# Attention row sums inverted on GpSimd by a power of minus one, in a fused attention and expert kernel

## Chip, cores and metric

The kernel runs on one core of one Trainium2 chip. The metric is the device time of one execution in microseconds (us). Before the change it is 942.04 us, the median of 3 runs (941.04 to 942.63).

## What is computed

```python
xn = layernorm(x)                                # x: 8 batches x 1024 tokens x 128
q, k = xn @ Wq.T + bq, xn @ Wk.T + bk            # 8 heads x 2
v = xn @ Wv.T + bv                               # 8 heads x 16
scores = leaky_relu(q @ k.T / sqrt(2), 0.2)      # per batch and head, 1024 x 1024
out = softmax(scores) @ v
y = x + (gamma * out + xn) + experts(xn)
```

`experts` is a top-2 routed layer of 16 experts with a capacity of 1024 tokens each; 12 of them are two matmuls with a gelu between. The change touches only the division of the softmax: each row of exponentials times values is divided by the sum of its exponentials.

## The kernel before

A prologue (0 to about 127 us) normalizes the tokens, projects q, k and v, routes the tokens and writes split bf16 parts of q and k to DRAM. Then attention and experts take turns: attention of batches 0 to 2, the 12 experts (about 365 to 540 us), attention of batches 3 to 7.

Attention is cut into 32 **passes** (`p`, 0 to 31): a pass is one batch, one group of 4 heads and one half (512) of its queries. A pass has 16 **units** (`i`): 8 chunks of 128 keys, and for each chunk two pairs of heads. One unit is a tile of 128 keys by 1024 (2 heads x 512 queries), in one of three slots of a ring in PSUM, and goes through four steps:

- `scores(i)`, TensorE, L825: two matmuls. It waits until the exponentials of unit i-3 have left the slot.
- `rectify(i)`, VectorE, L1133: max with 0 and a factor, in place in PSUM.
- `shifted(i)`, TensorE, L835: two matmuls that add the linear part and a shift onto it.
- `exponentials(i)`, ScalarE, L718: exp from the slot into SBUF (`pr`).

TensorE runs `shifted(i)`, `scores(i+2)`, and then `values` (L855), half of exponentials times values for the chunk before, in this order, unit by unit. `values` adds up into one of two PSUM banks (`acc`), 16 values and the row sum in each block of 32 rows, since the value tile has a column of ones.

When a pass is complete, VectorE does `turn(p)` (L1109): a 32x32 block transpose of `acc` into the SBUF tile `ot`, put ahead of `rectify` of the sixth unit (`TURN = 5`) of the pass after it. Ahead of the seventh it does `denominators(p)` (L1115): the reciprocal of the 16 row sums per partition, into `rg`. GpSimd then multiplies in `quotient(p)` (L439, `att`), and the sync engine's queue (SP) issues `spread(p)`: 16 small DMAs (L333, 8 KB each) that bring the blocks to their tokens in `moved`. One pass later GpSimd adds `moved` to `y` in `add_attention(p)` (L452), which `settle` calls. The last pass of each of the two attention parts (p = 11 and 31, `LAST`) goes another way: ScalarE copies `acc`, TensorE transposes it (L866), and VectorE's `finish` inverts (L1122) and multiplies (L1125) straight into `moved`. It does so before and after the change.

GpSimd's order is written out by hand, one program: in the first attention part `scatter` issues 128 indirect DMAs (L490, tokens to the experts' inputs), 11 or 12 in each pass but the last; in the second part `gather` issues 128 indirect DMAs (L505) and combines them (L518, L525), 4 or 8 a pass and none in the last. Each indirect DMA waits in `paced` for a certain unit's exponentials. In each pass, between these, stands `results`: `settle(p - 2)`, then `quotient(p - 1)`. So the quotient of a pass and all that follows on GpSimd are one queue. SP's queue is one too: operand loads (L312 to L314) every second pass, spreads, stores of finished batches to `out` (L323), and at the change to the experts `load_expert` (L357), which waits for all scatters. What TensorE needs first of the experts are the tokens of expert 0 and 1 (`turn_rows`, L898).

```python
                    def results():
                        ...
                        if p > first + 1:
                            settle(p - 2)
                        if p > first:
                            quotient(p - 1)
```

Of the kernel before, what the change touches and what calls it, by code (L numbers as in the profile page):

```python
# [8 lines left out]
ALU = mybir.AluOpType  # L9
# [3 lines left out]
P = 128  # L13
# [4 lines left out]
H, DV, DQ = 8, 16, 2  # L18
HG = 4
# [5 lines left out]
HALF = 512  # L25
# [29 lines left out]
UP = TB * PAIRS  # L55
# [5 lines left out]
TURN = 5  # L61
BLOCK = 32
NR = P // BLOCK
# [38 lines left out]
def build(nc, x, consts, w_qk, b_qk, w_vr, b_v, r_b, n_w, n_w_row, w1t, b1, w2t, b2, cvec, gamma, out):  # L102
# [4 lines left out]
    with ExitStack() as ctx:  # L107
        def sb(name, shape, dt=F32):
            return ctx.enter_context(nc.sbuf_tensor(name, shape, dt))

        def sem(name):
            return ctx.enter_context(nc.semaphore(name))
# [38 lines left out]
        vp = sb("vp", [P, NHG, TB, HG, 32])  # L151
        pr = sb("pr", [P, BUFS, HG, HALF])
        ot = sb("ot", [P, 2, HALF])
        rg = sb("rg", [P, 2, HALF // BLOCK])
        att = sb("att", [P, 2, NR, GT, DV])
        moved = sb("moved", [P, 2, HG, GT, DV])
        rowones = sb("rowones", [1, M], BF16)
# [42 lines left out]
                 "v_rdy y_upd hi_rdy rem_rdy mid_rdy lo_rdy scaled v_evac lg_rdy lgb_rdy parts_out0 parts_out1 dir_rdy ext_rdy "  # L200
                 "kmax_rdy bok_rdy hat1_rdy hat_rdy u_rdy ub_rdy shift_rdy shift_out0 shift_out1 "
                 "qz_init weighted at_rdy sum_rdy inv_rdy row_step route ones_rdy max_rdy off_rdy reset_rdy r_exp cnt_rdy pos_rdy ztile init_rdy kz_init "
                 "ld0 ld1 vp_rdy s1 relu s2 exps pv acc_evac o_rdy turned rg_rdy att_rdy spread0 spread1 y_att "
                 "scat staged pool_step carry "
                 "ed0 ed1 etr edt fc1 gel fc2 yo_rdy yo_out gath0 gath1 comb final").split()
        S = {n: sem(n) for n in names}
# [6 lines left out]
        def wait_done(engine, name, count):  # L213

            if not (isinstance(count, int) and count <= 0):
                engine.wait_ge(S[name], count)
# [27 lines left out]
        LAST = (BH * NPB - 1, B * NPB - 1)  # L244

        def quotients(p):

            return sum(k not in LAST for k in range(p + 1))

        def spreads(p):  # L250

            return sum(k not in LAST and k % 2 == p % 2 for k in range(p + 1))
# [137 lines left out]
        def _(pool):  # L390
            pool.memset(onesb[:], 1.0)
            pool.memset(ef[:, 3, :], 0.0).then_inc(S["ztile"], 1)
            pool.memset(rowones[:], -1.0)
            pool.memset(va[:, :, :, DV:DV1], 1.0)
            pool.memset(vp[:], 0.0).then_inc(S["init_rdy"], 1)
            pool.memset(kz[:].rearrange("p a e m -> p (a e m)").bitcast(F32), 0.0)
# [34 lines left out]

            def quotient(p):

                pool.wait_ge(S["rg_rdy"], p + 1)
                if p > 1:
                    wait_done(pool, f"spread{p % 2}", 16 * HG * NR * spreads(p - 2))
                rows = ot[:, p % 2, :].rearrange("p (t r c) -> p t r c", r=NR, c=BLOCK)[:, :, :, 0:DV]
                inv_rows = rg[:, p % 2, :].rearrange("p (t r) -> p t r", r=NR).unsqueeze(3)
                pool.tensor_tensor(att[:, p % 2, :, :, :].rearrange("p r t d -> p t r d"), rows,  # L439
                                   inv_rows.broadcast_to([P, GT, NR, DV]), ALU.mult).then_inc(S["att_rdy"], 1)  # L440

# [105 lines left out]
            def attention(b0, b1, move):  # L547
                first, last = b0 * NPB, b1 * NPB - 1
                for p in range(first, last + 1):
                    b = p // NPB  # L550

                    def results():

                        if p % NPB == 0:
                            value_rows(b, 1)
                        if p % NPB == NQ and b + 1 < B:
                            value_rows(b + 1, 0)
# [5 lines that stand above are left out]
                    move(p, results)  # L563
                settle(last - 1)
                settle(last)
# [376 lines left out]
        def _(dve):  # L942
# [161 lines left out]
            def turn(p):  # L1104

                dve.wait_ge(S["pv"], TB * (p + 1))
                if p > 1:
                    dve.wait_ge(S["att_rdy"], quotients(p - 2))
                dve.transpose(ot[:, p % 2, :], acc[p % 2]).then_inc(S["turned"], 1)  # L1109

            def denominators(p):

                dve.wait_ge(S["turned"], p + 1)
                rows = ot[:, p % 2, :].rearrange("p (q c) -> p q c", c=BLOCK)
                dve.reciprocal(rg[:, p % 2, :], rows[:, :, DV]).then_inc(S["rg_rdy"], 1)  # L1115

            def finish(p):

                dve.wait_ge(S["o_rdy"], 1 + LAST.index(p))
                rows = acc[p % 2].rearrange("p (t g c) -> p g t c", g=HG, c=BLOCK)  # L1120
                inv_rows = rg[:, p % 2, :].rearrange("p (g t) -> p g t", g=HG)
                dve.reciprocal(inv_rows, rows[:, :, :, DV]).then_inc(S["rg_rdy"], 1)  # L1122
                dve.wait_ge(S["rg_rdy"], p + 1)
                dve.wait_ge(S["y_att"], p - 1)
                dve.tensor_tensor(moved[:, p % 2, :, :, :], rows[:, :, :, 0:DV],  # L1125
                                  inv_rows.unsqueeze(3).broadcast_to([P, HG, GT, DV]), ALU.mult
                                  ).then_inc(S["turned"], 1)

            def rectify(i):

                dve.wait_ge(S["s1"], i + 1)
                s = ring[i % RING]
                dve.tensor_scalar(s, s, 0.0, 1.0 / SLOPE - 1.0, ALU.max, ALU.mult).then_inc(S["relu"], 1)  # L1133

            def attention(b0, b1, done=0):
                first, end = b0 * NUB, b1 * NUB
                for i in range(first + done, end):
                    if i % UP == TURN and i > first + UP:
                        turn(i // UP - 1)
                    if i % UP == TURN + 1 and i > first + UP:  # L1140
                        denominators(i // UP - 1)
                    rectify(i)
                finish(end // UP - 1)

            attention(0, BH)


# [15 lines left out]
            for i in range(BH * NUB, BH * NUB + RING):  # L1163
                rectify(i)
            expert_rows(E_MLP - 1, 1)
            attention(BH, B, RING)


# [52 lines left out]
```

## Time and profile before

| | before |
|---|---|
| median of 3 runs | 942.04 us (941.04 to 942.63) |
| span of the profiled execution | 940.0 us |
| run time less span (startup and end outside the trace) | 2.0 us |
| attention, first part, first to last rectify | 127 to 362 us |
| experts | 365 to 541 us |
| attention, second part, first to last rectify | 541 to 931 us |
| mean granted TensorE clock | 0.981 of full speed |
| DMA of an expert's tokens (512 KB), issue to landing | 4.9 us (median) |

The span is from the first to the last instruction of one execution that the profiler recorded; the page gives no run time for that execution by itself, so its own time is taken as 940.0 us of span and the 2.0 us around it. Engines are PE (TensorE), DVE (VectorE), ACT (ScalarE), POOL (GpSimd) and SP. A line of the timeline shows the start, the length, the engine, the source line, what is written from what, how many instructions are merged, and in brackets the idle time before and what is thought to have ended it.

### The profile page before, as it was taken

How to read it: one execution, taken by the hardware profiler on the slowest of the kernel's cores; microseconds unless marked ns; L12 is line 12 of the kernel's file. 1: busy time of each engine (PE TensorE's matmuls, PEld its weight loads, DVE VectorE, ACT ScalarE, POOL GpSimd, SP SyncE). 2: the span in 40 equal slices, each digit the busy share in tenths (PEclk: the TensorE clock that was granted, in tenths of full speed). 3: DMA queues.
4: the chain of work that ended last, by engine and by line, in shares of the span. 5: the costliest groups of instructions: out<-in, count | busy, mean ns of one | idle time of the engine just before them, and what ended most of it. 6: DMA issues, size and time to landing. Idle time of an engine off the chain costs nothing. (4 is left out here: it accounts for less than half of the span.)

```text
span 940.0 us, 20061 instructions
## 1 busy us (share of the span) xinstructions
PE 861.2 (92%) x7499; PEld 348.9 (37%) x7500; DVE 735.3 (78%) x859; ACT 691.3 (74%) x811; POOL 601.5 (64%) x610
## 2 busy tenths in 40 slices
PE   0688269999999999999999999999999999999997
PEld 0444112222222224776867732222222222222222
DVE  5788889999999994101011099999999999999996
ACT  0578888888888887444453568888888888888886
POOL 3355247777777663999999226657567575765782
PEclk9999659999999999999999999999999999999999
DMA  7833101111111112233242210102112111210202
GB/s 214 303 66 74 32 27 33 51 40 51 47 27 36 25 38 88 90 121 116 93 138 71 94 44 22 40 19 59 36 25 59 25 36 29 70 29 13 69 18 55
DMA packets 71225, 59.36 MB, mean 63 GB/s; under 512 B 33770, under 2 KB 58178, under 8 KB 71136
## 3 DMA queue, kind: packets, MB, share of 16 engines
q1 hardware_dynamic: 61520, 48.06, 17.6%
q0 software_dynamic: 8192, 9.37, 3.6%
q8 instruction: 55, 0.90, 0.4%
q10 hardware_dynamic: 1424, 0.76, 0.3%
q14 instruction: 34, 0.28, 0.1%
HBM read 31.58 MB, written 30.02 MB: 66 GB/s over the span
## 5 line engine op out<-in xcount | busy, mean ns | idle before, releaser
L1133 DVE TENSOR_SCALAR ps<-ps 128x1024 f32<-128x1024 f32 x512 | 600.1, 1224 | 14.6 <-PE ps L825 11.7
L718 ACT ACTIVATE pr<-ps 128x1024 f32<-128x1024 f32 x512 | 523.4, 1023 | 104.5 <-PE ps L835 72.9
L855 PE MATMUL ps<-pr,vp 128*32 128x256 f32 x4096 | 327.2, 392 | 0.1
L835 PE MATMUL ps<-q,kz 64*128 64x512 bf16 x1024 | 200.7, 389 | 10.2 <-DVE ps L1133 4.4
L825 PE MATMUL ps<-q,kz 62*128 62x512 bf16 x1024 | 200.3, 389 | 2.9 <-DMA q<-parts_dram 1.3
L505 POOL DMA_INDIRECT xs<-eout,idxs x128 | 129.0, 1008 | 105.0 <-ACT pr L718 75.5
L490 POOL DMA_INDIRECT disp<-xn,idx x128 | 125.9, 984 | 50.8 <-issue 29.2
L835 PEld LDWEIGHTS ps<-q,kz 64*128 64x128 bf16 x1024 | 49.0, 93 | 225.7 <-DVE ps L1133 188.4
L1152 DVE TENSOR_TENSOR pr<-ps,parts 128x1024 f32<-128x1024 f32 x12 | 14.7, 1225 | 149.6 <-PE ps L920 149.6
L855 PEld LDWEIGHTS ps<-pr,vp 128*32 128x32 f32 x4096 | 81.1, 108 | 119.4 <-issue 117.6
L744 ACT ACTIVATE pr<-ps,b1s 128x512 f32<-128x512 f32 x96 | 65.8, 687 | 53.7 <-PE ps L909 53.7
L920 PEld LDWEIGHTS ps<-w,pr 128*128 128x128 f32 x768 | 88.6, 192 | 6.2 <-issue 6.2
L920 PE MATMUL ps<-w,pr 128*128 128x128 f32 x768 | 89.8, 275 | 0.0
L825 PEld LDWEIGHTS ps<-q,kz 62*128 62x128 bf16 x1024 | 49.3, 93 | 107.1 <-ACT pr L718 76.3
L909 PE MATMUL ps<-pr,w 128*128 128x512 f32 x192 | 84.7, 593 | 0.0
L628 POOL TENSOR_TENSOR y<-y,xn x24 | 56.4, 2351 | 4.9 <-POOL xn L625 4.9
L525 POOL TENSOR_TENSOR y<-y,xs 128x256 f32<-128x256 f32 x64 | 46.5, 727 | 11.4 <-POOL y L525 5.7
L452 POOL TENSOR_TENSOR y<-y,moved 128x256 f32<-128x256 f32 x32 | 23.4, 731 | 45.1 <-DMA moved<-att 26.8
L909 PEld LDWEIGHTS ps<-pr,w 128*128 128x128 f32 x192 | 35.5, 190 | 40.2 <-issue 39.5
L404 POOL TENSOR_TENSOR ot<-pr,parts 112x512 f32<-112x512 f32 x16 | 18.7, 1170 | 38.1 <-ACT parts L674 38.0
L737 ACT ACTIVATE pr<-ps,nw 128x512 f32<-128x512 f32 x24 | 15.2, 683 | 37.4 <-PE ps L898 37.4
L518 POOL TENSOR_TENSOR xs<-xs,co 128x256 f32<-128x256 f32 x64 | 37.9, 618 | 0.6
(122 smaller groups left out, 530.3 us busy)
## 6 DMA issues: line engine op xcount, KB each, us to landing
moved<-att SPq DMA_DIRECT2D x480, 8.0 KB
disp<-pr SPq DMA_DIRECT2D x12, 512.0 KB, 4.9
eout<-pr SPq DMA_DIRECT2D x12, 512.0 KB, 2.9
y<-in_x SPq DMA_DIRECT2D x8, 512.0 KB, 8.1
out<-y SPq DMA_DIRECT2D x7, 512.0 KB
w<-in_w1t SPq DMA_DIRECT2D x12, 256.0 KB, 3.2
w<-in_w2t SPq DMA_DIRECT2D x12, 256.0 KB, 3.4
xs<-disp SPq DMA_DIRECT2D x6, 512.0 KB, 4.9
```

What stands on the lines that cost most here:

```text
L490: pool.indirect_dma_start(out=disp, out_offset=bass.IndirectOffsetOnAxis(ap=idx[:, k, s * TB + t:s * TB + t + 1], axis=0), in_=xn[:, s * T ...
L505: pool.indirect_dma_start(out=g1[:, g % 2, t, c, :], out_offset=None, in_=eout, in_offset=bass.IndirectOffsetOnAxis(ap=idxs[:, c, GB * i + ...
L525: pool.tensor_tensor(yt, yt, rows[:, :, c, :], ALU.add).then_inc(S["comb" if c else "weighted"], 1)
L628: pool.tensor_tensor(yb, yb, xb, ALU.add).then_inc(S["pool_step"], 1)
L718: act.activation(pr[:, c % BUFS, 2 * pair:2 * pair + 2, :], ring[i % RING], ACT.Exp, scale=SLOPE).then_inc(S["exps"], 1)
L744: act.activation(hs[:, f, half * HALF:(half + 1) * HALF], ps[:, 2 + n % 4, :], ACT.Gelu, bias=b1s[:, u, f:f + 1]).then_inc(S["gel"], 1)
L825: last = pe.matmul(ring[i % RING][:, k, :], kz[r:r + ONES, hg, pair, kc * P:(kc + 1) * P], q2[r:r + ONES, hg, qh * HALF:(qh + 1) * HALF], ...
L835: last = pe.matmul(ring[i % RING][:, k, :], kz[r:r + TILE, hg, pair, kc * P:(kc + 1) * P], q2[r:r + TILE, hg, qh * HALF:(qh + 1) * HALF], ...
L855: last = pe.matmul(acc[p % 2][32 * g:32 * g + 32, cols], vp[:, hg, kc, g, :], pr[:, c % BUFS, g % PAIRS * 2 + g // PAIRS, cols], start=(kc ...
L909: pe.matmul(ps[:, 2 + n % 4, :], w1[:, 2 * u * FFN + f * P:2 * u * FFN + (f + 1) * P], dt_[:, half * HALF:(half + 1) * HALF], start=True, ...
L920: mm = pe.matmul(o, hs[:, f, j * P:(j + 1) * P], w1[:, (2 * u + 1) * FFN + f * P:(2 * u + 1) * FFN + (f + 1) * P], start=(f == 0), stop=(f ...
L1133: dve.tensor_scalar(s, s, 0.0, 1.0 / SLOPE - 1.0, ALU.max, ALU.mult).then_inc(S["relu"], 1)
```

## The change

In `quotient`, GpSimd no longer waits for VectorE's reciprocal but for the transpose itself, forms the 16 reciprocals per partition as row sum to the power of a tile of minus ones, waits for that result, and multiplies as before. `denominators` is gone from VectorE's program. The reciprocal tile becomes one buffer for GpSimd (`rg`) and one for `finish` (`rl`), `minus` is filled once at the start, and `finish` counts its own semaphore.

```diff
-        rg = sb("rg", [P, 2, HALF // BLOCK])
+        rg = sb("rg", [P, HALF // BLOCK])
+        rl = sb("rl", [P, HALF // BLOCK])
+        minus = sb("minus", [P, HALF // BLOCK])
...
             pool.memset(rowones[:], -1.0)
+            pool.memset(minus[:], -1.0)
...
             def quotient(p):
 
-                pool.wait_ge(S["rg_rdy"], p + 1)
+                pool.wait_ge(S["turned"], p + 1)
                 if p > 1:
                     wait_done(pool, f"spread{p % 2}", 16 * HG * NR * spreads(p - 2))
                 rows = ot[:, p % 2, :].rearrange("p (t r c) -> p t r c", r=NR, c=BLOCK)[:, :, :, 0:DV]
-                inv_rows = rg[:, p % 2, :].rearrange("p (t r) -> p t r", r=NR).unsqueeze(3)
+                rows_sum = ot[:, p % 2, :].rearrange("p (q c) -> p q c", c=BLOCK)[:, :, DV]
+                pool.tensor_tensor(rg[:], rows_sum, minus[:], ALU.pow).then_inc(S["power"], 1)
+                pool.wait_ge(S["power"], quotients(p))
+                inv_rows = rg[:].rearrange("p (t r) -> p t r", r=NR).unsqueeze(3)
                 pool.tensor_tensor(att[:, p % 2, :, :, :].rearrange("p r t d -> p t r d"), rows,
                                    inv_rows.broadcast_to([P, GT, NR, DV]), ALU.mult).then_inc(S["att_rdy"], 1)
...
-            def denominators(p):
-
-                dve.wait_ge(S["turned"], p + 1)
-                rows = ot[:, p % 2, :].rearrange("p (q c) -> p q c", c=BLOCK)
-                dve.reciprocal(rg[:, p % 2, :], rows[:, :, DV]).then_inc(S["rg_rdy"], 1)
...
             def finish(p):
...
-                inv_rows = rg[:, p % 2, :].rearrange("p (g t) -> p g t", g=HG)
+                inv_rows = rl[:].rearrange("p (g t) -> p g t", g=HG)
                 dve.reciprocal(inv_rows, rows[:, :, :, DV]).then_inc(S["rg_rdy"], 1)
-                dve.wait_ge(S["rg_rdy"], p + 1)
+                dve.wait_ge(S["rg_rdy"], 1 + LAST.index(p))
...
                     if i % UP == TURN and i > first + UP:
                         turn(i // UP - 1)
-                    if i % UP == TURN + 1 and i > first + UP:
-                        denominators(i // UP - 1)
                     rectify(i)
```

## Rows read from the trace of the kernel before

**Rows 1.** The page, part 1: busy time of each engine

```profile
PE 861.2 (92%) x7499; PEld 348.9 (37%) x7500; DVE 735.3 (78%) x859; ACT 691.3 (74%) x811; POOL 601.5 (64%) x610
```

**Rows 2.** Groups by line, VectorE: instruction and count, busy us, mean ns, idle before

```profile
L1115 DVE RECIPROCAL rg<-ot 128x16 f32<-128x16 f32 x30 | 7.0, 233 | 0.0
```

**Rows 3.** Waits of the whole run: who waited for whom, total us, times, longest

```profile
PEld ps L835 <- DVE ps L1133: 188.4, 421, 4.5
```

**Rows 4.** Timeline of VectorE around one pass

```profile
704.14 0.71 DVE L1109 STREAM_TRANSPOSE ot<-ps 128x512 f32<-128x512 f32 x1
704.77 1.20 DVE L1133 TENSOR_SCALAR ps<-ps 128x1024 f32<-128x1024 f32 x1
705.88 0.23 DVE L1115 RECIPROCAL rg<-ot 128x16 f32<-128x16 f32 x1
706.03 17.58 DVE L1133 TENSOR_SCALAR ps<-ps 128x1024 f32<-128x1024 f32 x15
723.53 0.71 DVE L1109 STREAM_TRANSPOSE ot<-ps 128x512 f32<-128x512 f32 x1
```

**Rows 5.** Timeline of ScalarE around the same transpose

```profile
701.49 1.02 ACT L718 ACTIVATE pr<-ps 128x1024 f32<-128x1024 f32 x1 [0.20 <-PE ps L835]
...
703.89 1.02 ACT L718 ACTIVATE pr<-ps 128x1024 f32<-128x1024 f32 x1 [0.20 <-PE ps L835]
...
706.46 1.02 ACT L718 ACTIVATE pr<-ps 128x1024 f32<-128x1024 f32 x1 [0.37 <-PE ps L835]
707.73 2.16 ACT L718 ACTIVATE pr<-ps 128x1024 f32<-128x1024 f32 x2 [0.24 <-PE ps L835]
```

**Rows 6.** Timeline of TensorE's matmuls around the same transpose

```profile
702.89 0.64 PE L855 MATMUL ps<-pr,vp 128*32 128x256 f32 x8
703.46 0.39 PE L835 MATMUL ps<-q,kz 64*128 64x512 bf16 x2
...
706.03 0.39 PE L835 MATMUL ps<-q,kz 64*128 64x512 bf16 x2
...
706.57 0.64 PE L855 MATMUL ps<-pr,vp 128*32 128x256 f32 x8
707.30 0.39 PE L835 MATMUL ps<-q,kz 64*128 64x512 bf16 x2
```

**Rows 7.** Timeline of GpSimd over the last three passes

```profile
886.57 1.00 POOL L505 DMA_INDIRECT xs<-eout,idxs  x1 [2.31 <-ACT pr L718]
...
898.90 0.72 POOL L525 TENSOR_TENSOR y<-y,xs 128x256 f32<-128x256 f32 x1 [0.18 <-POOL y L525]
...
922.98 0.62 POOL L439 TENSOR_TENSOR att<-ot,rg 128x256 f32<-128x256 f32 x1
```

**Rows 8.** Timeline of SP's queue, from pass 27 to the end

```profile
857.06 10.91 SPq L333 DMA_DIRECT2D moved<-att  x16
...
883.40 1.13 SPq L323 DMA_DIRECT2D out<-y  x2
...
923.62 10.67 SPq L333 DMA_DIRECT2D moved<-att  x16
```

**Rows 9.** Timeline of the last 5 us: GpSimd's two last additions, VectorE's last product

```profile
935.58 1.46 POOL L452 TENSOR_TENSOR y<-y,moved 128x256 f32<-128x256 f32 x2 [11.99 <-issue]
935.75 0.42 DVE L1125 TENSOR_TENSOR moved<-ps,rg 128x256 f32<-128x256 f32 x1
```

**Rows 10.** Groups by line: a small product on GpSimd, a longer reciprocal on VectorE

```profile
L601 POOL TENSOR_TENSOR co<-pr 128x64 f32<-128x64 f32 x3 | 1.0, 322 | 0.2
L1158 DVE RECIPROCAL gsum<-gsum 128x64 f32<-128x64 f32 x1 | 0.5, 544 | 0.0
```

**Rows 11.** Waits of GpSimd in the first attention part, 160 to 346 us

```profile
POOL disp L490 <- ACT pr L718: 16.5, 26, 3.0
```

**Rows 12.** Timeline at the change to the experts: SP's load, TensorE's first use

```profile
367.13 0.43 SPq L357 DMA_DIRECT2D pr<-disp  x1
...
376.22 1.04 PE L898 MATMUL ps<-cst,pr 128*128 128x128 f32 x8
```

More of the change, by code:

```diff
@@ L202, in build @@
                  "qz_init weighted at_rdy sum_rdy inv_rdy row_step route ones_rdy max_rdy off_rdy reset_rdy r_exp cnt_rdy pos_rdy ztile init_rdy kz_init "
-                 "ld0 ld1 vp_rdy s1 relu s2 exps pv acc_evac o_rdy turned rg_rdy att_rdy spread0 spread1 y_att "
+                 "ld0 ld1 vp_rdy s1 relu s2 exps pv acc_evac o_rdy turned rg_rdy power att_rdy spread0 spread1 y_att "
                  "scat staged pool_step carry "
```

## Prediction

> **What bounds the kernel now.** I read the page's busy times first [rows 1]: TensorE leads with 92%, but its ends are modelled; VectorE shows 78% over the run, and in the timeline of a pass it has no gap at all [rows 4]. That invites the reading "VectorE is the bound, so whatever leaves it is won". The waits seem to agree: TensorE's weight loads for `shifted` waited 188.4 us, 421 times, "for VectorE" [rows 3]. So the next view has to be the timeline of one pass, engine by engine, and it says otherwise.
>
> Follow the exponentials [rows 5]. Two units apart they start at 701.49 and 703.89: 2.40 us. The exponential of unit 1 ends at 702.51, which lets `scores` of unit 4 go; `values` follows at 702.89, `shifted` of unit 3 at 703.46 [rows 6], its exponential at 703.89: 1.02 + 0.38 + 0.57 + 0.43 = 2.40. This loop holds ScalarE and TensorE only. It runs twice side by side, once for the odd units and once for the even, and both turn in 2.40 us, so a unit costs 1.20 us. VectorE's own pace is less than 1.20: the 15 rectifies from 706.03 take 17.58 us, 1.17 each, waits included. And the weight loads' wait "for VectorE", 188.4 / 421 = 0.45 us each, falls into the 0.57 us of `values` that stand ahead of `shifted`: what ended it was TensorE's own work, while VectorE had been done before.
>
> Only the transpose breaks into it. It is put before rectify 5 (odd loop): that rectify runs from 704.77 to 705.97, `shifted` follows at 706.03 and the exponential at 706.46 [rows 4 to 6], 2.57 us after the one of 703.89 instead of 2.40. The odd loop loses 0.17 us in each pass. Eight turns of 2.40 and 0.17 make 19.39 us, and that is what lies between two transposes: 723.53 - 704.14 = 19.39 [rows 4]. (Every second pass is 0.08 longer, by one more wait of TensorE at new operands.) So the pass is explained without the reciprocal.
>
> **VectorE: the reciprocal goes.** 30 instructions of 233 ns, 7.0 us busy [rows 2]. On VectorE's clock the next rectify moves from 706.03 to 705.88: 0.15 us, since they overlap. That one is rectify 6, in the even loop. It now ends at 707.24 and `shifted` takes it at 707.30; TensorE itself was free at 706.57 + 0.57 = 707.14 [rows 6]. The even exponential could come at about 707.58, not 707.73. But the odd one after it starts at 708.86, which is 706.46 + 2.40: its own loop sets it, not the even one (ScalarE still rests 0.11 us between the two). The even loop only follows at less distance. The pass length is set by the odd loop, at the transpose, where the reciprocal has no part. I take **0 us** for all 30. Bounds: nothing, and 0.15 x 30 = 4.6 us if it were passed on in full.
>
> **GpSimd: the power.** Each quotient becomes power, handover, product. What is added is d = length of the power + 0.18 us, the gap between two dependent instructions there (the row at 898.90) [rows 7]. No row shows a power. Below: as a plain product; 256 elements take 620 ns [rows 7] and 64 take 322 [rows 10], so 1.55 ns an element and 223 ns fixed: 0.25 us for 16. A gain is excluded, as it is one more instruction on a queue in order. Nearer to it: VectorE's reciprocal takes 544 ns for 64 and 233 for 16 [rows 2, 10], 6.5 ns an element against 1.2 of its rectify; the same factor on GpSimd gives 8.4 x 16 + 223 = 0.36 us. Above: the routine that GpSimd runs in software for an indirect DMA, 1.0 us [rows 7], and not quite two of them, 1.8 us, as the outer end. A power is a logarithm, a product and an exponential, so more than a reciprocal; I take **0.8 us**, nearer to the indirect DMA, and d = 1.0. The earlier start (GpSimd no longer waits for the reciprocal) is worth nothing: at 922.98 it comes to the product 3 us after the reciprocal.
>
> The Trainium skill, "GPSIMD Engine Reference", section "Performance versus the Vector engine", calls elementwise work on GpSimd about twice as slow as on VectorE and advises against moving it. By that the power would be 2 x 0.233 = 0.47 us and the sum below 2.5 us, still slower.
>
> **Where d is hidden.** In the middle of each part: GpSimd waits for paced units, and a quotient has a whole pass until the transpose after next needs its buffer. SP's spreads start later by the same, with 19.4 us a pass for 11 us of issue.
>
> **Where it isn't: the end.** The last stretch is a chain. Quotient 30 starts at 922.98; from 923.62 SP issues its 16 DMAs for 10.67 us [rows 8]; the last lands, and GpSimd adds at 935.58 [rows 9]. The other chain, by `finish`, has `moved` ready at 935.75 + 0.42 = 936.17. The second addition starts at 936.31, when the first is over. So delay of quotient 30 counts in full, but for 0.1 us. And GpSimd is without slack from 886.57 on, through quotients 28 and 29, two groups of gathers each, to 921 [rows 7]; its short wait for spread 29 moves along, since that spread starts with quotient 29. So 3 d. Before that GpSimd stood 2.31 us at 886.57, with exponentials long done; at 883.40 SP had issued two stores of 512 KB [rows 8], and they fill the DMA engines. Quotients 26 and 27 make GpSimd 2 d late there, which that pause takes up; but the stores stand in SP's queue behind the spread that began at 857.06 with the end of quotient 26, so the pause itself comes d later. That makes **4 d - 0.1 = 3.8 us**.
>
> **The first part.** 11 powers make GpSimd late by 11 d; its paced waits give back at most 16.5 - 26 x 0.3 (dispatch) = 8.7 us [rows 11]. Then the loads of expert 1 start late: tokens issued at 367.13, landing 4.9 us later, used at 376.22 [rows 12]: 4.2 us of slack. 11 d - 8.7 exceeds 4.2 only over d = 1.17, and then TensorE waits for the rest. With d = 1.0 nothing. The memset of `minus` (some 0.1 us before 10 us) and the semaphores of `finish`: 0, as GpSimd's first result is wanted tens of us later.
>
> **Sum.** 0 + 3.8 us on a span of 940.0: 943.8, and on the median (2.0 above the span) 945.8 us, 0.4% slower.
>
> **Rivals.**
> (a) *The power is short or the pause goes.* With 0.25 us, d = 0.43 and 4 d - 0.1 = 1.6 us. If the pause at 886.57 was an accident of the stores and disappears, 5 d - 2.2: with d = 0.8, 1.8 us. Either gives 942 to 943.9, within 0.2% (1.9 us), which is about what a measurement of this kernel can tell from no change. For it: plain products are that cheap. Chance 0.20.
> (b) *The power is long.* It decides from d = 1.17 on, at the loads of expert 1. Power 1.8 us, d = 1.98: 7.8 at the end and 21.8 - 12.9 = 8.9 at the experts: 16.7 us, 958.7. If it were some 20 us, GpSimd would bound every pass and the run would exceed 1200 us. For it: no row limits it. Chance 0.27.
> (c) *VectorE's time is given back.* If rectify 6 passed its 0.15 us on to the odd loop each pass, 4.6 us would be won against 30 places, and with a short power (1.6 us lost at the end) the result is 939.0: faster. It decides if the distance of the two loops, not the odd loop's own 2.40, set the exponential at 708.86. Against it: the 19.39 us come out without it. Chance 0.05.
> The forecast itself, powers of 0.35 to 1.0 us, 943.9 to 946.6: 0.48.
>
> **Numbers.** Range 942.0 to 959.0: from the pause gone to a power of 1.8 us; outside stay (c) and powers beyond. Faster 0.05, same 0.20, slower 0.75.
>
> **What would show it.** Right: no L1115; transposes still 19.39 and 19.47 apart; the exponential after the transposed rectify still 2.57 late; the even one at 1.11 behind the odd instead of 1.27; a new GpSimd row of 0.8 us x30 with 0.18 behind it; quotient 30 about 4 d later, the last addition as much. Wrong: transposes closer than 19.39 (then my loop is not what sets the pass), GpSimd's new row under 0.3 us or over 1.2 us, or TensorE idle at L898 near 376.

## The result and the profile after

The changed kernel takes 985.9 us (median of 4 runs, 984.54 to 988.96) against 941.5 (4 runs): a ratio of 1.0471, 95% interval 1.0446 to 1.0496. It is slower by 44 us, where 3.8 were forecast and 17 taken for the outer end of the range. The page of its profiled execution, its span, part 1 and the group of the new instruction (line, engine, what is written from what, count | busy us, mean ns | idle before it):

```profile
span 987.1 us, 20062 instructions
...
PE 865.6 (88%) x7499; PEld 349.7 (35%) x7500; DVE 731.8 (74%) x829; ACT 691.4 (70%) x811; POOL 690.6 (70%) x641
...
L442 POOL TENSOR_TENSOR rg<-ot,minus 128x16 f32<-128x16 f32 x30 | 88.3, 2942 | 0.0
```

GpSimd is busy 89 us longer than before [rows 1], and 88.3 of them are the power: **2.94 us** each, for 16 elements a partition. The product starts 3.02 us after the power (mean of 30), so the handover costs 0.08 us, not the 0.18 that were allowed for it. VectorE lost its 30 reciprocals, and its timeline answers to [rows 4]:

```profile
709.59 0.70 DVE L1115 STREAM_TRANSPOSE ot<-ps 128x512 f32<-128x512 f32 x1
710.22 18.94 DVE L1133 TENSOR_SCALAR ps<-ps 128x1024 f32<-128x1024 f32 x16
729.06 0.70 DVE L1115 STREAM_TRANSPOSE ot<-ps 128x512 f32<-128x512 f32 x1
```

The transposes are 729.06 - 709.59 = 19.47 us apart, exactly a long pass of before (the short ones are 19.39 again). No pass got shorter by the reciprocal that left it. ScalarE's timeline around the first of these transposes shows the same as [rows 5]:

```profile
709.34 2.15 ACT L724 ACTIVATE pr<-ps 128x1024 f32<-128x1024 f32 x2 [0.25 <-PE ps L841]
711.91 2.15 ACT L724 ACTIVATE pr<-ps 128x1024 f32<-128x1024 f32 x2 [0.42 <-PE ps L841]
```

The exponential of rectify 5, which the transpose delays, still comes 2.57 us after the one before it in its loop. Each row holds two exponentials, the second of which takes 1.02 us and ends at 2.15: it starts 1.13 us behind the first instead of 1.27, and the forecast had 1.11.

The 47.1 us between the two spans lie in two other places. The first is the change to the experts. TensorE's timeline after, to be set against its second transpose for the experts in [rows 12]:

```profile
361.05 1.07 PE L861 MATMUL ps<-pr,vp 128*32 128x256 f32 x16
381.34 1.94 PE L904 MATMUL ps<-cst,xs 128*128 128x128 f32 x8 [19.23 <-DMA xs<-disp]
383.21 1.59 PE L861 MATMUL ps<-pr,vp 128*32 128x256 f32 x16
```

and the first transpose of before, with the row that follows it there:

```profile
363.17 1.09 PE L898 MATMUL ps<-cst,xs 128*128 128x128 f32 x8
364.19 1.07 PE L855 MATMUL ps<-pr,vp 128*32 128x256 f32 x16
```

TensorE stands for 19 us, waiting for the tokens of expert 0. GpSimd's timeline in the first part tells why: it has next to no pauses left, and each quotient pushes all that follows it back by 3 us.

```profile
334.33 0.75 POOL L458 TENSOR_TENSOR y<-y,moved 128x256 f32<-128x256 f32 x1
335.01 2.95 POOL L442 TENSOR_TENSOR rg<-ot,minus 128x16 f32<-128x16 f32 x1
338.04 0.62 POOL L445 TENSOR_TENSOR att<-ot,rg 128x256 f32<-128x256 f32 x1
338.85 1.06 POOL L496 DMA_INDIRECT disp<-xn,idx  x1 [0.20 <-issue]
...
370.92 0.97 POOL L496 DMA_INDIRECT disp<-xn,idx  x1 [0.30 <-issue]
```

The last scatter ends at 371.9, not 347.1, and SP issues the tokens' DMA at 376.36 instead of 352.12: 24.2 us later. SP waits for two things of GpSimd there, one behind the other: quotient 9, whose spread it issues first, and then all scatters. Its rows tell which of them counts:

```profile
364.25 10.02 SPq L335 DMA_DIRECT2D moved<-att  x16
374.32 0.58 SPq L359 DMA_DIRECT2D w<-in_w1t  x1
...
376.36 0.43 SPq L359 DMA_DIRECT2D xs<-disp  x1
```

The loads of expert 0 start 0.05 us behind the last DMA of spread 9, as in the kernel before (350.03 and 350.07), while the last packet of a scatter landed at 373.1 (348.2 before). So it is SP's 10 us of issuing spread 9 that set the load; the scatters alone would have let it go 1.2 us earlier. Both stand behind the same ten quotients.

TensorE's slack takes 6 of the 24.2 us. It also comes back cold, as the windows show (stretch, length, then busy us of PE, PEld, DVE, ACT and POOL with counts, granted clock, DMA share, GB/s):

```profile
363.00:381.00 18.00, 0.00 (x0) 0.00 (x0) 0.00 (x0) 0.00 (x0) 11.33 (x11) 0.62 0.27 73
381.00:384.00 3.00, 2.66 (x16) 1.97 (x20) 0.00 (x0) 1.36 (x2) 0.00 (x0) 0.50 0.08 14
384.00:392.00 8.00, 8.00 (x32) 3.73 (x25) 1.14 (x3) 6.41 (x11) 0.00 (x0) 0.98 0.08 13
```

After 18 us without a matmul the granted clock is 0.50, the lower of the two levels (1.2 of 2.4 GHz). The 8 transposes take 1.94 us instead of 1.09, the 16 matmuls of `values` after them 1.59 instead of 1.07: 1.4 us for the clock. It is back at the upper level in the stretch from 384. For the tokens of expert 1 TensorE then waits again, and the granted clock falls again:

```profile
398.09 1.97 PE L904 MATMUL ps<-cst,pr 128*128 128x128 f32 x8 [2.20 <-DMA pr<-disp]
399.85 4.48 PE L926 MATMUL ps<-w,pr 128*128 128x128 f32 x32
```

```profile
398.00:400.00 2.00, 1.91 (x9) 1.92 (x10) 0.00 (x0) 0.69 (x1) 1.75 (x2) 0.50 0.00 0
```

In the kernel before the transposes took 1.04 us [rows 12] and the matmuls behind them 3.74, without a wait: 1.7 us more for the clock. From the last rectify of the first part to the first of the second it is 203.8 us, before 179.1: 24.7 more, of which the two waits (19.2 and 2.2) and the clock (1.4 and 1.7) make 24.5. Counted from the start of the execution the second part begins 23.6 us later, since the first ended 1.1 us earlier in this one.

The second place is the end. GpSimd's rows answer to [rows 7] and [rows 9]:

```profile
967.76 2.94 POOL L442 TENSOR_TENSOR rg<-ot,minus 128x16 f32<-128x16 f32 x1
970.77 0.62 POOL L445 TENSOR_TENSOR att<-ot,rg 128x256 f32<-128x256 f32 x1
982.71 1.40 POOL L458 TENSOR_TENSOR y<-y,moved 128x256 f32<-128x256 f32 x2 [11.32 <-issue]
```

The last rectify ends at 956.1, and the span ends at 987.1. Those 31.0 us were 8.7 before (931.3 to 940.0): 22.3 us more. Quotient 30 starts its product 28.1 us after its transpose, before 5.2 us. 23.6 us before the second part, 22.3 at its end and 1.2 on the way (in the first pass of the second part) make the 47.1.

### The profile page after: what moved, and what is told of

The parts are those of the page before. It is cut to its first block and busy times, and to the rows that moved or that the text cites. A ratio compares the mean times of both kernels' runs of the same rounds, so it can differ in the third digit from the quotient of the medians.

```text
span 987.1 us, 20062 instructions
## 1 busy us (share of the span) xinstructions
PE 865.6 (88%) x7499; PEld 349.7 (35%) x7500; DVE 731.8 (74%) x829; ACT 691.4 (70%) x811; POOL 690.6 (70%) x641
## 5 line engine op out<-in xcount | busy, mean ns | idle before, releaser
L442 POOL TENSOR_TENSOR rg<-ot,minus 128x16 f32<-128x16 f32 x30 | 88.3, 2942 | 0.0
L458 POOL TENSOR_TENSOR y<-y,moved 128x256 f32<-128x256 f32 x32 | 23.3, 730 | 44.0 <-DMA moved<-att 29.8
```

Of the source, the lines that this page charges most:

```text
L442: pool.tensor_tensor(rg[:], rows_sum, minus[:], ALU.pow).then_inc(S["power"], 1)
```

## Experiments

The theory after the result (A): GpSimd's queue carries the whole loss, by the length of the power, at these two places, and the reciprocal on VectorE was free. The rival (B): part of it comes from VectorE's side, from its order of work or from the waits that changed.

### The reciprocal taken away, nothing in its place

```diff
-                pool.wait_ge(S["rg_rdy"], p + 1)
+                pool.wait_ge(S["turned"], p + 1)
...
-                inv_rows = rg[:, p % 2, :]...
+                inv_rows = ones16[:]...
...
-                    if i % UP == TURN + 1 and i > first + UP:
-                        denominators(i // UP - 1)
```

> The kernel before without its 30 reciprocals on VectorE and with nothing in their place: GpSimd multiplies by ones, so the attention rows of 30 passes stay undivided. Theory A (GpSimd's queue carries the whole loss, the reciprocal on VectorE was free): transposes still 19.39 and 19.47 us apart, time within 1 us of 941.5. Theory B (VectorE's time was worth its 0.15 us a place): 937 us.

941.8 us, ratio 1.0007 (0.9997 to 1.0017). The timeline of VectorE:

```profile
704.41 0.70 DVE L1111 STREAM_TRANSPOSE ot<-ps 128x512 f32<-128x512 f32 x1
705.04 18.84 DVE L1135 TENSOR_SCALAR ps<-ps 128x1024 f32<-128x1024 f32 x16
723.79 0.70 DVE L1111 STREAM_TRANSPOSE ot<-ps 128x512 f32<-128x512 f32 x1
```

723.79 - 704.41 = 19.38. Seven us of VectorE's busy time are gone and the pass is as long as before. B has nothing to give back.

### The power beside the reciprocal

```diff
+                rows_sum = ot[:, p % 2, :].rearrange("p (q c) -> p q c", c=BLOCK)[:, 0:16, DV]
+                pool.tensor_tensor(spare[:, 0:16], rows_sum, minus[:, 0:16], ALU.pow)
                 inv_rows = rg[:, p % 2, :]...
```

> The kernel before with its reciprocals on VectorE kept and used, and GpSimd forming the same power beside them into a tile that nobody reads, ahead of each product, without a wait. Theory A: GpSimd's queue is 2.9 us longer in each of 30 quotients, and nothing else is needed: 982 to 986 us, as the changed kernel but for the handover of 0.08 us. Theory B (a good part comes from what changed on VectorE and in the waits, not from the length of the power): under 965 us.

982.5 us, ratio 1.0429 (1.0408 to 1.045). VectorE works as before, the result of the power is thrown away, and nearly the whole loss is there. The 3.4 us to the changed kernel go with the handover, in the main: there the product starts 3.02 us after the power, here 2.93, and 0.09 for each of 10 quotients ahead of the experts' load and of 19 ahead of the end make 2.7. In the profiled run TensorE also doesn't wait for expert 1 here (its transposes take 1.09 us, at the upper clock). How much of the 3.4 us is which wasn't measured.

### The power in one part only

```diff
+                if p < BH * NPB:
+                    pool.tensor_tensor(rg[:], rows_sum, minus[:], ALU.pow).then_inc(S["power"], 1)
...
+                else:
+                    pool.wait_ge(S["rd_rdy"], quotients(p) - powers(p))
```

(The run for the second part has `p >= BH * NPB`.)

> The changed kernel with the power on GpSimd in passes 0 to 10 only; passes 12 to 30 take their reciprocals from VectorE as before. Theory A with two separate places of loss (late scatters hold the first expert's tokens, 24 us; a late last quotient, 22 us): 962 to 967 us, TensorE idle about 19 us before its first expert transpose, the tail after the last rectify back at 9 us. Rival (the lag of the first part runs on into the second, or the second part's lag alone makes the loss): over 975 or under 950.

965.5 us, ratio 1.0256 (1.024 to 1.0272). TensorE waits 18.90 us for the first tokens, and the tail, from the end of the last rectify to the end of the span, is 9.1 us:

```profile
361.15 1.07 PE L871 MATMUL ps<-pr,vp 128*32 128x256 f32 x16
381.12 1.94 PE L914 MATMUL ps<-cst,xs 128*128 128x128 f32 x8 [18.90 <-DMA xs<-disp]
```

> The changed kernel with the power on GpSimd in passes 12 to 30 only; passes 0 to 10 take their reciprocals from VectorE. Theory A: no idle TensorE at the change to the experts, tail after the last rectify about 31 us instead of 9: 962 to 966 us. Together with the run of the first part alone the two losses add up to the whole, 44 us, within 3. Rival (the parts are coupled): they don't add up.

966.3 us, ratio 1.0253 (1.0236 to 1.0269). TensorE's first expert transpose comes 1.4 us after the last rectify of the part, as before, and the tail is 31.9 us. The two losses, 23.9 and 24.6 us, add up to 48.5, 4 more than the whole, a little outside the 3 that were allowed. In the profiled run of the second part the first rectify came at 131.0 us, 3.9 later than before, ahead of any power. Neither the cause of that nor that of the 4 us is known. Counted where they arise, in the profiled runs: from the last rectify of the first attention part to the first of the second 179.1 us before, 201.7 with the power in the first part, 180.0 with it in the second; the tails are 8.7, 9.1 and 31.9. The losses are 22.6 and 23.3 us, each in its own place but for 0.9 and 0.4 us: they are separate, as A has it. The changed kernel had 24.7 at the first place. With the power in the first part alone TensorE waits only 1.59 us for expert 1, and its clock doesn't fall a second time (these transposes take 1.09 us).

### What a power costs

```diff
             attention(BH, B, gather)
...
+            for op, n in PRICES:
+                col += n
+                pool.tensor_tensor(pc[:, col - n:col], pa[:, 0:n], pb[:, 0:n], getattr(ALU, op)).then_inc(S["pool_step"], 1)
```

> The kernel before, with ten more products on GpSimd behind its last addition: powers and plain multiplications of 1, 4, 16, 64 and 256 elements a partition, tile by tile, values 3.0 to the power of -1.0. Read for the length of each only. If the power is a routine with a cost per element, 16 take 2.9 us as in the changed kernel, 64 near 11 and 256 over 40, and 1 takes little over a multiplication. If it is a fixed cost (code, a table, a call), all five powers lie near 2.9 us. The multiplications should lie on 0.22 us and 1.55 ns an element.

It ran once (996.4 us), and only lengths are read from it. The groups by shape on that line hold one power and one multiplication each (busy is their sum, the mean is over both):

```profile
L646 POOL TENSOR_TENSOR price<-price 128x1 f32<-128x1 f32 x2 | 0.8, 386 | 0.0
L646 POOL TENSOR_TENSOR price<-price 128x4 f32<-128x4 f32 x2 | 1.2, 608 | 0.0
L646 POOL TENSOR_TENSOR price<-price 128x16 f32<-128x16 f32 x2 | 3.1, 1551 | 0.0
L646 POOL TENSOR_TENSOR price<-price 128x64 f32<-128x64 f32 x2 | 10.8, 5422 | 0.0
L646 POOL TENSOR_TENSOR price<-price 128x256 f32<-128x256 f32 x2 | 41.9, 20970 | 0.0
```

Taken singly from the trace, the powers of 1, 4, 16, 64 and 256 elements take 0.592, 1.024, 2.891, 10.537 and 41.227 us, the multiplications 0.179, 0.192, 0.211, 0.308 and 0.712. By the first and the last of these a power costs some **0.43 us and 160 ns an element** of each partition (2.99 us for 16, measured 2.89), a multiplication 0.18 us and 2.1 ns. The price is in the elements, not in a call or a load. Only one pair of values, 3.0 and -1.0, was timed here; the real row sums take 2.94 us for 16.

### Smaller doses

The edit of the power beside the reciprocal, with 4 and with 8 elements. It gives the size that the prediction had assumed and asks whether the rest of its sum holds.

> The kernel before with a power of 4 elements a partition beside each product on GpSimd, into a tile nobody reads. By the run of prices it takes 1.02 us, so each quotient is 0.99 us longer, the size that the prediction took for the change. If only the price of the power was wrong in the prediction, its sum holds here: nothing at the experts, 4 x 0.99 - 0.1 = 3.9 us at the end, 945.4 to 945.8 us. If the model of GpSimd's slack was wrong too, over 948.

947.3 us, ratio 1.007 (1.0055 to 1.0085): 6.4 us over the 940.9 of the kernel before, not 3.9.

> As before, with 8 elements a partition: 0.43 + 8 x 0.160 = 1.7 us for the power, 1.68 us longer in each quotient. The prediction's sum gives 4 x 1.68 - 0.1 = 6.6 at the end and 11 x 1.68 - 12.9 = 5.6 at the experts, together 12.2: 953.9 us, with TensorE idle some 5 us ahead of its first transposes for the experts. If the pauses that should take up lateness in passes 24 to 27 are used up already, the end costs 8 us or more and the time lies over 956.

956.6 us, ratio 1.0167 (1.0153 to 1.0181): 15.7 us, not 12.2. So the sum is short by 2.5 to 3.5 us even at small sizes. At the end 5.0 and 7.8 us were lost (tails of 13.7 and 16.5 against 8.7), where the sum has 3.9 and 6.6; at the experts, from last rectify to first, 1.3 and 9.0, where it has 0 and 5.6. Two of GpSimd's rows with 4 elements show two of the causes:

```profile
332.04 0.97 POOL L495 DMA_INDIRECT disp<-xn,idx  x1 [4.48 <-ACT pr L723]
```

```profile
889.32 1.00 POOL L510 DMA_INDIRECT xs<-eout,idxs  x1 [2.29 <-ACT pr L723]
```

The second is the pause that stood at 886.57 [rows 7]. SP's stores were then issued at 885.67, GpSimd is 2.75 us later, and the pause is as long as ever. In the changed kernel it is there too, at 925.36 with 2.29 us, five us after the stores (920.35). It stays at that place of GpSimd's own program and takes up no lateness, so the end pays for five quotients (26 to 30) and not four. A quotient is 1.03 us longer with 4 elements: 5 x 1.03 = 5.2, and the tail grew by 5.0. With 8 elements it is 7.8 of 5 x 1.66 = 8.3 us. In the changed kernel it is 22.3, and five quotients are only 5 x 3.02 = 15.1: there the pauses ahead of pass 26 are used up as well. Before, ten pauses of 1.8 to 5.2 us ahead of indirect DMAs lie between 670 and 855 us; in the changed kernel none over 1.4 us lies between 644 and 925.

The first row's pause is of the same kind. It was 2.98 before; here it is 4.48, with 8 elements 2.93, and in the changed kernel, with GpSimd some 20 us late, it is still 3.01, at 348.10. The three others over 1 us of that part, 1.18, 2.15 and 1.49 us, are gone in all late kernels. So the first part gives back some 3 to 6 us: the product of quotient 9 starts 6.7 us late where ten quotients had added 10.3, 11.6 where they had added 16.6, and 24.8 where they had added 30.2. 8.7 had been allowed.

The third cause is the clock. After the wait of 5.88 us with 8 elements the 8 transposes, the 16 matmuls of `values` and the 4 first ones of the expert take 1.94, 1.94 and 3.14 us, against 1.09, 1.07 and 1.98 before: 2.9 of the 9.0 us.

What makes the two lasting pauses is open; no run was made for it. SP's stores are near the one at the end in every run that was read for it: they were issued 3.0 to 5.5 us before it ended. A part of theirs isn't excluded, but its length, 2.29 to 2.31 us, doesn't follow them.

### What does set the pass

The first section of the prediction stands on VectorE's transpose reaching into one loop. If so, a transpose in pieces that stay inside VectorE's slack must shorten the pass by the 0.17 us.

```diff
-                dve.transpose(ot[:, p % 2, :], acc[p % 2]).then_inc(S["turned"], 1)
+                dve.transpose(ot[:, p % 2, 0:HALF // 2], acc[p % 2][:, 0:HALF // 2])
...
+                dve.transpose(ot[:, p % 2, HALF // 2:HALF], acc[p % 2][:, HALF // 2:HALF]).then_inc(S["turned"], 1)
...
+                    if i % UP == TURN + 1 and i > first + UP:
+                        turn_rest(i // UP - 1)
+                    if i % UP == TURN + 2 and i > first + UP:
                         denominators(i // UP - 1)
```

> The kernel before with the 128x512 transpose of each pass on VectorE cut into two of 128x256, ahead of the sixth and the seventh rectify, and the reciprocal one unit later. A test of what sets the pass. Theory A (the transpose delays one loop by 0.17 us in each of 30 passes, because 0.63 us is more than VectorE's slack, and the reciprocal's 0.15 us stays inside it): each half costs about 0.36 us and fits, so that the transposes come 19.2 and 19.3 us apart and the time falls by about 5 us to 936 to 938. Theory B (the pass is set by the sum of VectorE's work): no gain, 941 to 943 us.

943.5 us, ratio 1.0025 (1.0014 to 1.0035): a miss, and slower. First rectifies of passes are 19.44 and 19.53 us apart, 0.05 or 0.06 more than before, which over 30 passes makes most of the 1.8 us. The halves and the reciprocal on VectorE:

```profile
703.62 0.44 DVE L1109 STREAM_TRANSPOSE ot<-ps 128x256 f32<-128x256 f32 x1
703.99 1.20 DVE L1137 TENSOR_SCALAR ps<-ps 128x1024 f32<-128x1024 f32 x1
705.10 0.43 DVE L1113 STREAM_TRANSPOSE ot<-ps 128x256 f32<-128x256 f32 x1
705.45 1.20 DVE L1137 TENSOR_SCALAR ps<-ps 128x1024 f32<-128x1024 f32 x1
706.56 0.23 DVE L1119 RECIPROCAL rg<-ot 128x16 f32<-128x16 f32 x1
```

and ScalarE:

```profile
705.78 1.02 ACT L718 ACTIVATE pr<-ps 128x1024 f32<-128x1024 f32 x1 [0.27 <-PE ps L835]
707.14 1.02 ACT L718 ACTIVATE pr<-ps 128x1024 f32<-128x1024 f32 x1 [0.34 <-PE ps L835]
708.40 2.16 ACT L718 ACTIVATE pr<-ps 128x1024 f32<-128x1024 f32 x2 [0.24 <-PE ps L835]
```

The exponential of unit 5, at 705.78, is in time. The next one of its loop is 2.62 later, at 708.40: rectify 7 had 0.36 + 0.36 + 0.15 = 0.87 us of other work ahead of it, and VectorE makes up only some 0.08 us a unit (its rectifies start 1.12 us apart where nothing stands between them, against 1.20). What counts is the sum of its lateness at each rectify against a slack, which is estimated at 0.46 us, since 0.63 us of transpose cost 0.17: 0.87 - 2 x 0.08 - 0.46 = 0.25 us, and the row shows 0.22. The next run sets the halves further apart, ahead of rectifies 5 and 9 (`turn_rest` is the one above):

```diff
-                    if i % UP == TURN + 1 and i > first + UP:
+                    late = i // UP != B * NPB - 1
+                    if i % UP == TURN + (4 if late else 1) and i > first + UP:
+                        turn_rest(i // UP - 1)
+                    if i % UP == TURN + (6 if late else 2) and i > first + UP:
                         denominators(i // UP - 1)
```

> The kernel before with the transpose of a pass cut into two of 128x256 ahead of rectifies 5 and 9, the reciprocal ahead of rectify 11 (for the last pass of all 5, 6 and 7, as the end waits for it). In the run with the halves next to each other VectorE's lateness added up over three rectifies and passed its slack of some 0.4 us. Theory A (a loop is late only when VectorE's lateness exceeds that slack; it makes up 0.07 us a unit): no loop loses, transposes 19.2 and 19.3 us apart, 0.17 us saved in 29 passes, 936.5 to 938.5 us. Theory B (every 0.1 us put on VectorE costs the pass something): no change or slower, 941 to 945 us.

**937.4 us**, ratio 0.9962 (0.9945 to 0.9978): faster than both kernels, with more busy time on VectorE per transpose (0.44 + 0.43 us against 0.71). First rectifies of passes are 19.21 and 19.29 us apart, against 19.39 and 19.47; eight turns of 2.40 are 19.2. The 3.5 us are less than 0.18 in each of 30 passes: in the profiled run the first pass of the second part is 1.3 us longer than before (22.60 against 21.32), and why wasn't looked for. VectorE's timeline from one first half:

```profile
720.07 0.44 DVE L1109 STREAM_TRANSPOSE ot<-ps 128x256 f32<-128x256 f32 x1
720.43 4.59 DVE L1137 TENSOR_SCALAR ps<-ps 128x1024 f32<-128x1024 f32 x4
724.93 0.43 DVE L1113 STREAM_TRANSPOSE ot<-ps 128x256 f32<-128x256 f32 x1
725.29 2.33 DVE L1137 TENSOR_SCALAR ps<-ps 128x1024 f32<-128x1024 f32 x2
727.53 0.24 DVE L1119 RECIPROCAL rg<-ot 128x16 f32<-128x16 f32 x1
```

## Why the prediction was right and wrong

- **VectorE's reciprocal is worth 0**: right, by the run without it (1.0007) and by passes of 19.39 and 19.47 after. The reading of [rows 4 to 6] held, its 2.57 us included, though narrower than it was put: rectify 7 came just in time. Transpose and reciprocal put 0.78 us ahead of it; by the estimate of the slack above that is 0.16 us too late, and its loop is 0.17 us behind already. With 0.87 us, in the run with adjacent halves, it was late. Rival (c) is out.
- **The price of the power**: this is the step that failed. 0.8 us was taken, between a plain product (0.25) and an indirect DMA (1.0), with 1.8 us for the outer end; it is 2.94, and d is 3.02 instead of 1.0. The argument scaled VectorE's reciprocal to GpSimd and named a row of another kind as a ceiling. No row bounded the price from above, as rival (b) said, and the range still ended at 1.8. The right mechanism was (b), whose chance was 0.27.
- **The Trainium skill's** factor of two in "GPSIMD Engine Reference", section "Performance versus the Vector engine", would give 0.47 us, an estimate; the measured ratio to VectorE's 0.233 us is 12.6. Its advice not to move elementwise work there agrees with the result, its figure doesn't reach this operation.
- **The sum at the true price**: with d = 3.02 the prediction's own terms give 12.0 us at the end and 20.3 at the experts, 32.3 of the 44. The first is further off: the pause at 886.57 was taken to move with SP's stores, but moves with GpSimd, and at 3 us the pauses before it are used up too (22.3 us). The second was nearer (24.7 us): 8.7 us of slack were allowed where 3 to 6 exist, and of the 3.1 us of clock nothing was in the sum. At d = 1 the first two errors alone are worth 2.5 us.
- **Places**: right in the main. The end is late by quotient 30 and its 16 DMAs, the experts by the late loads. The load that holds TensorE first is that of expert 0, by SP's spread of quotient 9; the prediction looked at expert 1 alone, whose tokens cost 2.2 us of waiting more. Nothing in between moved by more than 1.2 us.

## What to carry to other kernels

An operation of which the trace has no row has no ceiling from rows of other kinds; measure it behind the last instruction of the kernel for a few sizes, or let the range run to where its engine would bound. A pause in an ordered queue is slack only if it shrinks when the queue is late; where the named releaser was done long before, as at 886.57, don't count it. And on an engine that looks full, place matters before amount: 7 us of work removed gave nothing, while more work in smaller pieces gave 3.5 us.

## What was unexpected of the hardware

GpSimd's power costs 160 ns an element of each partition beside 0.43 us, some 76 times the 2.1 ns of a multiplication. After 18 us without matmuls TensorE ran at the granted clock of 0.50 for its first 3 us and cost 1.4 us more on top of the wait. With only 5.88 us of waiting (8 elements) the first transposes took 1.94 us too, and in the changed kernel the 2.20 us of waiting for expert 1 were followed by a granted clock of 0.50 as well. With 1.24 us (4 elements) and with 1.59 (power in the first part) they took 1.06 and 1.09:

```profile
368.95 1.94 PE L903 MATMUL ps<-cst,xs 128*128 128x128 f32 x8 [5.88 <-DMA xs<-disp]
```

```profile
364.19 1.06 PE L903 MATMUL ps<-cst,xs 128*128 128x128 f32 x8 [1.24 <-DMA xs<-disp]
```
